# The last attention's inputs: all queries first, the class chain beside keys and values, values copied out of PSUM by ScalarE

## The reference, cut to what matters

```python
x = x + tanh(g_ffn[1]) * _L1_ffn_ref(_layernorm(x), g_info, W_qkv, W_proj, b_proj)
# _L1_ffn_ref, H = 16 heads of D = 16, REG = 5 register tokens:
qkv = (x @ W_qkv)                        # q, k, v of every token
q_n  = q_pure / norm(q_pure)             # every head of the tokens behind the registers
qg_n = q_g / norm(q_g)                   # q_g from g_info
sim  = (qg_n * q_n).sum(-1).mean(-1)     # one number a token
sim  = (sim - sim.min()) / (sim.max() - sim.min())
pos  = sim > 0.9                         # the class of a token
# attention in which a token sees the registers and the tokens of its own class;
# the registers' output is the mean of both classes'; then @ W_proj + b_proj
```

## Time and profile before

| | us |
|---|---|
| median of 3 runs (lowest, highest) | 1362.31 (1358.96, 1364.53) |
| the profiled execution's own time | 1365.11 |
| its span | 1363.4 |
| granted TensorE clock over the span, share of full | 0.949 |
| PE busy | 1227.1 (90%) |
| DVE busy | 1007.0 (74%) |
| ACT busy | 840.5 (62%) |
| POOL busy | 219.5 (16%) |

### The profile page before, as it was taken

One profiled execution on the slowest core, in us unless ns is written; L12 is line 12 of the kernel. 1 busy time (PEld: TensorE's weight loads), 2 busy tenths in 40 slices (PEclk: granted clock), 3 DMA queues, 4 the chain that ended last, 5 costly groups with the idle time before them and its releaser, 6 DMA issues.

```text
span 1363.4 us, 26337 instructions
## 1 busy us (share of the span) xinstructions
PE 1227.1 (90%) x10562; PEld 573.1 (42%) x10562; DVE 1007.0 (74%) x1499; ACT 840.5 (62%) x1468; POOL 219.5 (16%) x167
## 2 busy tenths in 40 slices
PE   4988993999998999487999999999999999999978
PEld 3566682555557555133332233332323323233237
DVE  4896587565537555456899999999999999999703
ACT  2233383677751555111787787878878788787871
POOL 2120024455642233107000000000000000000000
PEclk8877895999999999688999999999999999999999
DMA  6100016576600233306154423543334432343003
GB/s 185 26 1 15 1 22 113 113 132 124 110 2 1 70 134 122 108 15 95 38 85 78 56 58 66 85 74 61 61 61 85 77 57 62 62 85 49 2 1 124
DMA packets 78825, 92.55 MB, mean 68 GB/s; under 512 B 15210, under 2 KB 53356, under 8 KB 78704
## 3 DMA queue, kind: packets, MB, share of 16 engines
q1 hardware_dynamic: 78704, 90.87, 33.2%
HBM read 67.02 MB, written 23.80 MB: 67 GB/s over the span
## 4 chain that ended last, share of the span: by engine, by line
PE 60%; DVE 29%; ACT 5%; issue 2%; DMA 1%; SPq 1%; POOL 1%; DVEq 0%; ACTq 0%; POOLq 0%
DVE sm L1986 19%; PE ps L1486 10%; PE ps L1477 9%; PE ps L1458 6%; PE ps L1377 4%; ACT W L991 3%; PE ps L1276 2%; PE ps L1596 2%; PE ps L1267 2%; PE ps L1268 2%; PE ps L1194 2%; PE ps L1384 2%; PE ps L1413 2%; PE ps L1325 2%; PE ps L1468 1%
## 5 line engine op out<-in xcount | busy, mean ns | idle before, releaser
L1986 DVE TENSOR_REDUCE sm<-ps 128x1 f32<-128x1024 f32 x512 | 599.8, 1218 | 31.2 <-PE ps L1458 27.9
L991 ACT ACTIVATE W<-ps 128x512 f32<-128x512 f32 x1024 | 534.8, 605 | 138.5 <-PE ps L1486 134.5
L1486 PE MATMUL ps<-R 99*32 99x512 bf16 x4096 | 317.8, 383 | 6.3 <-ACT W L991 3.2
L1477 PE MATMUL ps<-W,R 128*32 128x512 f32 x2048 | 265.3, 594 | 0.7 <-ACT W L991 0.7
L1486 PEld LDWEIGHTS ps<-R 99*32 99x32 bf16 x4096 | 86.1, 94 | 224.4 <-ACT W L991 168.1
L779 POOL COPY R<-R 128x512 f32<-128x512 f32 x16 | 10.2, 642 | 589.3 <-PE ps L1477 589.3
L1458 PE MATMUL ps<-R 50*128 50x512 bf16 x512 | 88.9, 388 | 15.5 <-DVE sm L1986 12.7
L1458 PE MATMUL ps<-KM,R 50*128 50x512 bf16 x512 | 87.2, 384 | 9.7 <-DVE sm L1986 6.7
L919 ACT ACTIVATE R<-ps 77x512 f32<-77x512 f32 x128 | 75.0, 592 | 24.5 <-PE ps L1268 15.3
L1477 PEld LDWEIGHTS ps<-W,R 128*32 128x32 f32 x2048 | 63.0, 111 | 42.2 <-ACT W L991 1.4
L1804 DVE TENSOR_REDUCE small<-ps 128x4 bf16<-128x308 f32 x128 | 57.5, 473 | 24.0 <-PE ps L1234 23.8
(11 more groups left out here) (258 smaller groups left out, 1589.6 us busy)
## 6 DMA issues: line engine op xcount, KB each, us to landing
R<-x_parts SPq DMA_DIRECT2D x96, 128.0 KB, 4.9
R<-q_parts SPq DMA_DIRECT2D x192, 64.0 KB
R<-q_parts SPq DMA_DIRECT2D x96, 128.0 KB
R<-k_parts SPq DMA_DIRECT2D x96, 128.0 KB
x_parts<-R SPq DMA_DIRECT2D x8, 768.0 KB, 6.8
q_parts<-R SPq DMA_DIRECT2D x24, 256.0 KB, 2.6
k_parts<-R SPq DMA_DIRECT2D x24, 256.0 KB, 2.6
X<-in_x SPq DMA_DIRECT2D x4, 1024.0 KB, 10.2
```

The source lines that it names most:

```text
L991: act.activation(PR[:, s % 2, h, :], third_bank("score", 64 * u + n), ACT.Exp, scale=0.25).then_inc(s_sfree, 1)
L1477: mm = pe.matmul(bank(7)[32 * h:32 * h + 32, :], VST[j][:, k, h, :], PR[:, s % 2, h, :], start=(k == 0), stop=(k == TB - 1))
L1486: mm = pe.matmul(o[32 * c:32 * c + 32, :], KST[j][0:MAX_ROW + 1, h, t:t + 32], QST[j][0:MAX_ROW + 1, h, 512 * (s // 8):512 * (s // 8) + 51 ...
L1986: dve.tensor_reduce(MX[:, half, h, q:q + 1], bank(2 * ((p + 1) % 2), 2), AX, ALU.max).then_inc(s_tfree, 1)
```

## The change

- The transposes are no longer a stage by themselves: `transposes3(c + 1)` stands in front of chunk c's query projection, all through one pair of banks (4). The transposed chunks go to `R2`, the keys `KT` to `R1` (they changed places).
- The statistics of the last batch move behind the first two query chunks; the q_g chain moves ahead of the third residual and into its first batch.
- A first loop makes the queries of all chunks, in two pairs of banks by turns (2 and 6), with the sums for the classes. ACT makes h straight from PSUM, DVE copies q out of PSUM (`s_qf`), and subtracts h from PSUM's copy.
- A second loop makes keys (pairs 4 and 2) and values (pair 6). ACT makes h of k from PSUM and copies the values out (four copies a chunk); DVE copies k and subtracts from PSUM, and runs a piece of the class chain (`class_chain(c)`) behind each of chunks 0 to 5, the root being ACT's after chunk 1's values; PE's three small products stand behind chunks 3, 4 and 5.
- The parts have two sets of buffers by turns for the queries, then for the keys, before one for each kind; SP writes the query parts first, then the key parts, between which it issues the other loads.

Core of the diff (SP and PE; DVE and ACT follow the same order):

```diff
-            for c in range(NC):
-                sp.wait_ge(s_ql, c + 1)
-                ... 3 writes of QP
-                sp.wait_ge(s_kl, c + 1)
-                ... 3 writes of KP
+            for c in range(NC):
+                write_qk(QP, c, s_ql, s_qw)
...
+            for c in range(3):
+                write_qk(KP, c, s_kl, s_kw2)
...
             load_max_parts(0, 0)
+            for c in range(3, 6):
+                write_qk(KP, c, s_kl, s_kw2)
             sp.wait_ge(s_sc2, CLS_DONE)
             ... 16 writes of the class rows
+            write_qk(KP, 6, s_kl, s_kw2)
             ... load of the row for the register scores
             sp.wait_ge(s_clw, 16 * 3 * B)
             load_max_class_rows(0, 0)
+            write_qk(KP, 7, s_kl, s_kw2)
+            ... wait for all key parts
+            load_parts(0, 0)
             load_max_stacks(1, 1)
```

```diff
+            transposes3(0)
+            for c in range(NC):
+                if c + 1 < NC:
+                    transposes3(c + 1)
+                pe.wait_ge(s_xt, NC * 2 + c + 1)
+                if c >= 2:
+                    pe.wait_ge(s_qr, c - 1)
+                projection(q_pair(c), 0, c)
                 if c >= 2:
                     sim_transposes(c - 2)
                 if c >= 1:
                     sim_products(c - 1)
+            for c in range(NC):
+                if c >= 2:
+                    pe.wait_ge(s_krs, c - 1)
+                projection(k_pair(c), 1, c)
+                if c == 0:
+                    sim_transposes(NC - 2)
+                    sim_products(NC - 1)
+                else:
+                    pe.wait_ge(s_vf, c)
+                value_projection(c)
+                ... the three products of the class chain behind c = 3, 4, 5
```

ACT and DVE in the first loop, chunk c:

```diff
+                if c + 1 < NC:
+                    transpose_copy(c + 1)
+                act.copy(PB2[:, c % 2, 0], q).then_inc(s_qh, 1)
+                act.wait_ge(s_qf, c + 1)
                 act.activation(Qsq[:, c % 2], Qf[:, c % 2], ACT.Square)
                 if c >= 1:
                     copy_sums(c - 1)
+                act.copy(PB2[:, c % 2, 1], resQ[:, c % 2]).then_inc(s_qm, 1)
...
+                dve.tensor_copy(Qf[:, c % 2], q).then_inc(s_qf, 1)
+                dve.tensor_tensor(resQ[:, c % 2], q, PB2[:, c % 2, 0], ALU.subtract)
```

More of the change, by code:

```diff
@@ L365, in build_program @@
         s_kl = sem("k_part_l")
-        s_qw = sem("q_parts_written")
-        s_kw2 = sem("k_parts_written")
+        s_qw = [sem(f"q_parts_written{n}") for n in range(2)]
+        s_kw2 = [sem(f"k_parts_written{n}") for n in range(2)]
         s_qrr = sem("register_queries_kept")
@@ L970, in _ @@
-            act.activation(rn2, rn2, ACT.Sqrt).then_inc(s_rp, 1)
+                act.wait_ge(s_qr, c + 1)
+                act.copy(PB2[:, c % 2, 1], resQ[:, c % 2]).then_inc(s_qm, 1)
+            for c in range(NC):
+                act.wait_ge(s_qp, NC + 2 * c + 1)
+                if c >= 2:
+                    act.wait_ge(s_kw2[c % 2], 48 * (c // 2))
+                else:
+                    act.wait_ge(s_qw[c % 2], 48 * (NC // 2))
+                act.copy(PB2[:, c % 2, 0], k_pair(c).rearrange("p (j t) -> p j t", j=2)).then_inc(s_kh, 1)
+                if c == 0:
+                    copy_sums(NC - 1)
+                act.wait_ge(s_krs, c + 1)
+                act.copy(PB2[:, c % 2, 1], resK).then_inc(s_km, 1)
+                act.wait_ge(s_qp, NC + 2 * c + 2)
+                if c == 0:
+                    act.wait_ge(s_ql, NC)
+                b, t = c // 2, 4 * (c % 2)
+                for g in range(4):
+                    vv = act.copy(V2[:, 4 * b + g, t:t + 4, :],
+                                  bank(6, 2).rearrange("p (i n) -> p i n", i=4)[:, :, 64 * g:64 * g + 64])
+                vv.then_inc(s_vf, 1)
+                if c == 1:
+                    act.wait_ge(s_smk, 2 * NC)
+                    act.activation(rn2, rn2, ACT.Sqrt).then_inc(s_rp, 1)
@@ L1315, in _ @@
             transposes1(0)
+            pe.wait_ge(s_qc, 2)
+            pe.matmul(bank(6)[:, 0:2], BBm, qg2, start=True, stop=True).then_inc(s_qk, 1)
             for c in range(NC):
@@ L1942, in _ @@
+            for c in range(NC):
+                k = k_pair(c).rearrange("p (j t) -> p j t", j=2)
+                dve.wait_ge(s_kh, c + 1)
+                dve.tensor_copy(KT[:, :, 512 * c:512 * c + 512], k).then_inc(s_kf, 1)
+                if c >= 1:
+                    dve.wait_ge(s_kl, c)
+                else:
+                    dve.wait_ge(s_sim, NC)
+                dve.tensor_tensor(resK, k, PB2[:, c % 2, 0], ALU.subtract).then_inc(s_krs, 1)
+                class_chain(c)
             assert ch[0] == CLS_DONE
+            dve.wait_ge(s_qp, 3 * NC)
```

314 lines of the change are left out of this document (164 added, 150 removed).

## The result

| | median us (runs) | ratio to the kernel before, 95% interval |
|---|---|---|
| before | 1362.55 (4) | |
| changed | 1347.61 (4) | 0.9891 [0.9867, 0.9915] |
| changed, second chip | 1347.06 (5) | 0.9862 [0.9839, 0.9885] |

The change gains 15 us (18 to 19 on the second chip), where 28 were forecast: 1347.6 lies 13.6 over the predicted 1334, outside its range by 0.6. The profiled execution of the changed kernel took 1347.31 us with a span of 1345.6. Against the profiled one of before that is 17.8 less; that execution of before lay 2.8 over 1362.31, the median that the prediction went by.

A forecast was written before the change was run, and what follows sets the result against it. PE bounds the projections; gains lie in its idle stretches before and after: 26.9 us by the first tile, 2.2 for the clock, less 0.5 to 1, gives 28, a median of 1334.3 (8 in 10: 1326 to 1347).

The forecast's parts named there:

- key part 3: Second loop: SP's 18 loads make this part's write some 3.7 us late, costing 0 to 1 us.
- 4.4, hidden: First loop: DVE's normalising, copy, subtraction and small copies total 4.4 us per chunk, hidden under rounds of about 6.0.
- some 1.4 us behind PE's end: End of second loop: DVE finishes subtracting k(7) and laying out register queries then; register scores start at 543.9.
- ACT's ring: First loop: ACT's cycle of copies, h, square, sums and m takes 6.0 us per chunk against PE's 5.9.
- At full clock a round is 1.00 + 0.33 … four are 5.3: First register scores: four rounds at full clock take 5.3 us, first tile at 549.2, 26.9 us earlier.
- left two ends open and took the middle: Second register scores: gain 31.2 us at full clock or 26.9 at half clock; 29 was taken.
- The stall behind the reciprocal: Second loop: the root and the 3.37 us reciprocal delay DVE's copy of k(2), so PE waits 2.5 us for values 2.
- 8 x 3.45: Second loop's end: PE's remaining projections from 509.9, plus 1.5 for the chain's products, end at 542.5.
- The rings bind: Rival, 17%: first-loop rounds of 6.8 us cost 6, slow value copies and late parts another 7; gain 15, 1347 us.
- Nothing waits: Rival, 8%: no reciprocal stall and full clock, PE ends at 539.2; gain 34, 1328 us.
- The wait comes back elsewhere: Rival, 4%: late key parts on SP delay the scores' row load, 22 of the 28 us gone; 1356 us.
- Slower: Rival, 4%: PE at half clock through the first loop, 46 us over if in every round; 1380 us.

The follow-up runs named there:

- chain_behind: The changed kernel with the class chain put back behind the second loop, all else as changed; 1367.61 us, ratio 1.0010 to the kernel before.
- half_subtraction: The changed kernel with POOL's subtraction for the third part made over 512 of its 1024 columns, the rest zeroed once; 1340.56 us, ratio 0.9817 to the kernel before.
- norm_ahead: The changed kernel with chunks 3 and 4 normalised one round earlier, ahead of the last batch's statistics; 1345.65 us, ratio 0.9851 to the kernel before.
- queries_early: The changed kernel with register queries laid out before chunk 7's keys and the scores' row loaded ahead of key part 6; 1341.57 us, ratio 0.9831 to before.
- keep_clock: The changed kernel with unread matmuls on PE, 14 ahead of the first register scores and 9 ahead of the second; 1341.05 us, ratio 0.9825 to before.
- loads_between: The changed kernel with SP's 18 loads split, 12 behind key part 0 and 6 behind key part 2; 1351.89 us, ratio 0.9886 to the kernel before.

## Why the prediction was wrong

The direction and the main reason were right: the gain comes from the class chain and its trip lying in front of the scores (chain_behind). The size was off, by these steps; "predicted" is the prediction's own figure, measured is the first profiled execution.

| step | predicted | measured | over |
|---|---|---|---|
| first projection | 436.5 | 437.0 | 0.5 |
| end of PE's values | 542.5 | 545.45 | 3.0 (with the 0.5) |
| from there to the scores | 1.4 | 3.50 | 2.1 |
| first scores to tile 1 | 5.3 | 8.4 | 3.1 |
| tile 1 to tile 2 | 10.3 | 11.33 | 1.0 |
| tile 2 to the loop, against before | 0 | 54.85 − 52.73 | 2.1 |

Together 11.3. The 0.5 to 1 that the sum took off for key part 3 is in the second row already, which leaves about 10.5, for the 10.2 by which the span gained less than 28 (17.8).

**The failed step is "4.4, hidden" for DVE in the first loop**, and its like at the end, "some 1.4 us behind PE's end". Both took operations of DVE at their free length. The prediction had weighed the port against POOL for operations with two SBUF inputs only, in the class chain. The normalising has one tensor input, reads and writes SBUF, and is held as well: 3.17 and 2.93 against 1.36, and two rounds took 8.2 and 7.0, over the 6.5 that the prediction named as a sign of being wrong. half_subtraction shows the cause, norm_ahead the price (3.0 to 3.4 us). Some 0.85 of it (the estimate under half_subtraction) is the statistics' own, for which the prediction had allowed 1.1 "once; ACT's ring covers it": it did not cover it. The laying out of the register queries does have two SBUF inputs; it was simply not asked what POOL does at that moment. The Trainium skill (VectorE: DVE Perf Modes, Mode 2×_2P) lists a fp32 tensor-with-scalar operation from SBUF among those that use both read ports for one tensor, and the Trainium skill (SBUF — State Buffer, SBUF: two separate sides) says that such a mode takes the pair shared with GpSimd. The trace agrees for POOL's subtraction, so the pages would have named this operation. For POOL's inverse root it does not: beside that (1.94 us at 430.42 in the changed kernel) each normalising operation took 0.41, as alone.

**The second failed step (3.1 in the table, and the 1.0 below it) is "At full clock a round is 1.00 + 0.33 … four are 5.3"**, which took no gap between values and scores into account: with 3.5 us of idle the clock fell within the scores. queries_early and keep_clock both bring the 5.3, one by removing the gap, the other by filling it. For the second scores the prediction left two ends open and took the middle; of the executions in which the wait for exp (1.84 to 2.27 us) was not filled, all but half_subtraction's and chain_behind's had them at half clock for a part. The last row of the table, where the forecast had zero, goes with the prologue's mean clock, 0.88 against 0.94 in before. It is no step of the change: with the same instructions from tile 2 to the loop, the kernels without unread matmuls there took from 52.7 to 56.7 us.

**Right, step by step.** The start at 437.0. The first loop's steady round, 5.9 with PE as its bound (6.0 by ACT's ring). The stall behind the reciprocal, 1.84 (2.5). The end of the second loop: the prediction writes "8 x 3.45" from 509.9 on, but its 542.5 needs nine, and nine projections are what runs behind the fourth values' wait; the figure is right, the count is a slip. Key part 3: ACT waits 3.77 for it, about the 3.7 by which the part was forecast late, and PE 0.75 (0 to 1); SP's twelve loads held up the queue for 6.99. The chain's small operations beside POOL: two of 1.96 and 2.10 in DVE's slack, with no wait behind them. The value copies: 0.36 to 0.40 us each, as forecast, but they start 0.26 apart, so that four take 1.19, between the bounds 0.85 and 2.3, where the prediction added them up to 1.45.

**The rivals.** "The rings bind" named 1347, and 1347 came, but by chance and not by it: PE was busy all of 26.3 us in the steady part of the first loop, no ring of ACT bound, and late parts cost PE 0.75, not 7. "Nothing waits" was wrong by the waits above. "The wait comes back elsewhere" did not occur (loads_between moves 1 us). "Slower" neither: the clock was 1.00 from 437 to 545.5, in spite of the waits of 2.66 and 1.01.

**Open.** When the clock falls within a gap of 2 to 3.5 us was not settled; executions of the same kernel differ by 1.5 us in the first scores and by 1.6 in the second. Nor is it shown why the clock is lower at the ends of the last 722 to 725 us in some executions.

## What to carry to other kernels

When work is moved, lay each of DVE's operations against what POOL does at the new time, not only against DVE's own slack. Here multiplications, subtractions, copies and operations of a tensor with a scalar, from SBUF to SBUF, ended only behind POOL's subtraction when they started while it ran; statistics, reductions and copies out of PSUM did not, and can be put there instead, as norm_ahead does with the statistics. Moving the latency chain in front of the long work was worth 15 to 19 us here, and three small moves, two of them out of the way of POOL, another 11. An idle gap of 3.5 us on PE was paid twice here, once as the gap and again as half clock behind it (one of 2.27 in most executions, but not in all), so the last operation ahead of a dependent stage is the one to bring forward.

## What the runs showed of the hardware that was not expected

- DVE's normalising (128x256, one tensor input, SBUF to SBUF) is held by POOL's subtraction for as long as that runs (3.17 us against 1.36; 2.21 with a subtraction of 1.16). Its copies out of PSUM are not: 1.22 to 1.23 with 1.02 of it beside POOL, 1.21 to 1.23 alone. Nor are the statistics (0.41 to 0.42 beside it, 0.40 to 0.42 alone), though they go from SBUF to SBUF. Its subtractions out of PSUM never met POOL's in these runs.
- A DVE operation of 32 columns took 1.96 and 2.10 us beside POOL, 0.18 free of it.
- PE fell to half clock behind a wait of 2.27 us after more than 100 us at full clock (queries_early), and behind the same wait in another execution did not (half_subtraction).
- ACT's copies of 256 columns out of PSUM take 0.36 to 0.40 us each and start 0.26 us apart (four in 1.19).
